# Autocorrelation decoder layer: the top-8 weights chosen by comparison with the raw correlation, with the order of the pair pipeline rewritten

## What is computed

```
qf, kf = fft(q), fft(k)                      # over the 64 positions
corr = ifft(qf * conj(kf)).real              # 64 lags for each head and channel
w, idx = top_k(corr, 8)                      # int(2 * log(64)) = 8
w = softmax(w)
out = sum_i w_i * v[min(idx_i + pos, L - 1)]
x = layernorm(x + out)
...
e = clip(floor(log2(max(|v|, 2**-10))), 0, 2); step = 2 ** (e - 1)
q = clip(round(|v| / step) * step, 0, 6) * sign(v)
```

## Time and profile before

| | |
|---|---|
| median of 3 executions | 321.19 us (321.08 to 324.42) |
| the profiled execution | 323.65 us |
| its span, first to last instruction | 321.6 us |
| TensorE busy, share | 274.6 us, 85% |
| VectorE | 269.8 us, 84% |
| ScalarE | 231.1 us, 72% |
| GpSimd | 174.7 us, 54% |
| mean granted TensorE clock | 0.978 |

### The profile page before, as it was taken

One profiled execution on the slowest core, in us unless ns is written; L12 is line 12 of the kernel. 1 busy time (PEld: TensorE's weight loads), 2 busy tenths in 40 slices (PEclk: granted clock), 3 DMA queues, 4 the chain that ended last, 5 costly groups with the idle time before them and its releaser, 6 DMA issues.

```text
span 321.6 us, 4437 instructions
## 1 busy us (share of the span) xinstructions
PE 274.6 (85%) x1060; PEld 109.8 (34%) x1060; DVE 269.8 (84%) x871; ACT 231.1 (72%) x541; POOL 174.7 (54%) x226
## 2 busy tenths in 40 slices
...
GB/s 207 396 273 354 325 160 213 128 23 65 36 33 85 78 0 17 116 1 2 2 0 16 17 14 6 50 49 18 51 34 51 51 16 51 34 50 49 51 82 99
DMA packets 22576, 26.54 MB, mean 83 GB/s; under 512 B 10771, under 2 KB 11411, under 8 KB 22550
## 3 DMA queue, kind: packets, MB, share of 16 engines
...
...
## 4 chain that ended last, share of the span: by engine, by line
DVE 30%; ACT 20%; PE 18%; issue 15%; POOL 11%; DMA 3%; SPq 1%; POOLq 0%; DVEq 0%; ACTq 0%
DVE big L1172 5%; DVE m L1153 4%; DVE X L1107 3%; DVE big L1142 3%; DMA big<-in_xT_dram 3%; PE ps L380 3%; ACT big L654 3%; DVE ps L1203 3%; ACT L752 2%; DVE ps L1081 2%; ACT X L682 2%; PE ps L562 2%; POOL big L925 2%; POOL big L931 2%; DVE big L1277 2%
## 5 line engine op out<-in xcount | busy, mean ns | idle before, releaser
L654 ACT ACTIVATE big<-X,lnv 128x512 f32<-128x512 f32 x48 | 34.2, 713 | 15.0 <-DVE X L1107 15.0
L1107 DVE SCALAR_TENSOR_TENSOR X<-ps,X 128x512 f32<-128x512 f32 x48 | 32.1, 682 | 10.7 <-PE ps L415 6.1
L391 PE MATMUL ps<-ctx_ring,consts 64*128 64x512 f32 (+1 forms) x96 | 35.8, 643 | 0.0
L441 PEld LDWEIGHTS ps<-consts,big 96*128 96x128 f32 x256 | 29.8, 191 | 13.4 <-issue 10.6
L441 PE MATMUL ps<-consts,big 96*128 96x64 f32 x256 | 32.0, 278 | 1.1 <-DVE big L1142 1.1
L1184 DVE TENSOR_TENSOR big<-ps,ctxf 128x512 f32<-128x512 f32 x48 | 30.8, 683 | 2.0 <-PE ps L475 1.3
L682 ACT ACTIVATE X<-X,lnv 128x512 f32<-128x512 f32 x32 | 25.8, 808 | 0.6
L1172 DVE MATCH_REPLACE8 big<-w,big 128x64 f32<-128x64 f32 x128 | 25.1, 210 | 0.0
L838 POOL TENSOR_TENSOR big<-big 128x512 f32<-128x512 f32 x4 | 5.8, 1444 | 35.5 <-DVE big L1250 25.5
L918 POOL TENSOR_TENSOR big<-big 128x512 f32<-128x512 f32 x15 | 19.0, 1268 | 6.2 <-DVE big L1172 6.0
L1142 DVE TENSOR_TENSOR big<-ps,ctxf 96x512 f32<-96x512 f32 x32 | 20.4, 677 | 0.8 <-PE ps L428 0.8
...
## 6 DMA issues: line engine op xcount, KB each, us to landing
...
```

The source lines that it names most:

```text
L391: mm(bank(LANE_BANK[lane]), mat((CY_0, CY_1, CY_C)[f])[half, :], ctx_ring[half, r * N:(r + 1) * N], start=True, stop=True).then_inc(s_cfor ...
L441: last = mm(ps[:, 2 * N + j * P + b * L:2 * N + j * P + (b + 1) * L], PQ[0:EVEN, b * N + j * P:b * N + (j + 1) * P], mat(IC_E)[0:EVEN, 0:L ...
L654: squared[k, n] = chain(a(JUNK[k], row(n), ACT.Square, bias=st[:, 0:1], scale=-float(V), accum_out=st[:, 2:3]))
L1107: stt(row(m), bank(b), 0.0, row(m), ALU.add, ALU.add, accum_out=st[:, 0:1]).then_inc(s_sum[k], 1)
```

## The change

The two loops in the diff are those of TensorE and GpSimd. The maxima and the mask now come from the raw correlation. match_replace reads CR and m8 instead of G and w8 and writes TAKEN (-3e38) where one of the 8 maxima stands; it can run before the exponentials. GpSimd no longer subtracts anything from G: it only negates the shift, and ScalarE takes exp(CR - shift) in eight instructions of 64 columns, one a group, with the shift as bias. VectorE forms WN as (REST == TAKEN) * G in one scalar_tensor_tensor. Of the rounding, the exponent mask stays on VectorE, now a tensor_tensor with a broadcast column `field` from SBUF to SBUF, and the maximum and product with MAGIC move to GpSimd. w8 goes. All the loops are written in a new order with other offsets, and with another list of idle products.

```diff
-DRAIN_BUSY = ((0, 4), (6, 6), (5, 3))
+DRAIN_BUSY = {LAST + 6: 10, LAST + 7: 12}
+TAKEN = -3.0e38
+EXPONENT = 0x7F800000
...
+            for t in range(1, PAIRS + 9):
+                out_rest(t - 6)
+                weights_to_time(t - 5)
+                out_even(t - 6)
+                weight_rest_forms(t - 5)
+                weight_forms(t - 5)
+                projection(t)
...
+                correlation(t - 3)
+                quantized_to_channels(t - 8)
+                feed_forward(t - 8)
+                query_forms(t - 2)
+                if t in DRAIN_BUSY:
+                    pe.wait_ge(s_sum[0], PAIRS)
+                    kept_busy(DRAIN_BUSY[t])
...
-                    a(w8[:, :], w8[:, :], ACT.Exp).then_inc(s_g, 1)
-                    a(G, G, ACT.Exp).then_inc(s_g, 1)
+                    for g in range(NG):
+                        last = a(G[:, g * L:(g + 1) * L], CR[n % 2][:, g * L:(g + 1) * L], ACT.Exp,
+                                 bias=den[:, 3 * NG + g:3 * NG + g + 1])
+                    last.then_inc(s_g, 1)
...
-                    chain(g_.tensor_tensor(groups(w8[:, :], TOP), top, sh.broadcast_to([P, NG, TOP]), ALU.subtract))
-                    g_.tensor_tensor(groups(G, L), groups(CR[n % 2], L), sh.broadcast_to([P, NG, L]),
-                                     ALU.subtract).then_inc(s_gs, 1)
+                    g_.tensor_scalar(den[:, 3 * NG:4 * NG], sh, -1.0, None, ALU.mult).then_inc(s_gs, 1)
...
-                    g_.tensor_tensor(WN, G, REST, ALU.subtract).then_inc(s_wn, 1)
...
+                    pool.wait_ge(s_expo, n + 1)
+                    chain(g_.tensor_scalar(MB, MB, 0.25, MAGIC, ALU.max, ALU.mult))
...
+            for t in range(PAIRS + 9):
+                block_scaled(t - 4)
+                finished(t - 9)
+                differences(t - 1)
+                clamped(t - 4)
+                rounded_off(t - 4)
                 top_differences(t)
...
-                        last = v_.match_replace(REST[:, g * L:(g + 1) * L], w8[:, g * TOP:(g + 1) * TOP],
-                                                G[:, g * L:(g + 1) * L], 0.0)
+                        last = v_.match_replace(REST[:, g * L:(g + 1) * L], top[:, g * TOP:(g + 1) * TOP],
+                                                CR[n % 2][:, g * L:(g + 1) * L], TAKEN)
...
-                    do(ts(bank(1).bitcast(I32), VB.bitcast(I32), 0x7F800000, None, ALU.bitwise_and))
-                    ts(MB, bank(1), 0.25, MAGIC, ALU.max, ALU.mult).then_inc(s_magic[1], 1)
+                    tt(MB.bitcast(I32), VB.bitcast(I32), field[:, 0:1].broadcast_to([P, V]), ALU.bitwise_and
+                       ).then_inc(s_expo, 1)
...
+                    stt(WN, REST, TAKEN, G, ALU.is_equal, ALU.mult).then_inc(s_wn, 1)
```

More of the change, by code:

```diff
@@ L355, in stored @@
                     sp.dma_start(pair_rows(out, n // 2, n % 2), row(n)).then_inc(s_store, 16)
-            for n in range(PAIRS + 3):
+            for n in range(PAIRS + 5):
                 quantized_to_channels(n)
-                stored(n - 3)
+                stored(n - 5)
             sp.wait_ge(s_store, 16 * PAIRS)
@@ L773, in weight_channels @@
                 a(wqT[:, :].rearrange("p (c n) -> p c n", c=VC)[:, :, bass.ts(l, P)],
-                  bank(4 if l == VC - 1 else 2).bitcast(BF16)[:, 0:V].rearrange("p (c n) -> p c n", c=VC), ACT.Copy).then_inc(s_qe[0], 1)
+                  bank(7 if l == VC - 1 else 2).bitcast(BF16)[:, 0:V].rearrange("p (c n) -> p c n", c=VC), ACT.Copy).then_inc(s_qe[0], 1)
             for m in range(SLOTS + 1):
                 slot(m)
-            for t in range(PAIRS + 10):
-                squares(0, t)
-                corr_out(t - 3)
-                if t == 3:
-                    weight_channels(VC - 1)
-                squares(2, t - 9)
-                if t == 2:
+            for t in range(PAIRS + 8):
+                if t == 1:
                     act.wait_ge(s_mlp, SLOTS)
                     a(SQ_LAST, XC[1], ACT.Square, bias=base[:, DEPTH:DEPTH + 1]).then_inc(s_sq1, 1)
-                quantized_out(t - 7)
-                factors(0, t - 1)
-                top_exponentials(t - 3)
-                weights_out(t - 4)
-                log_sum(t - 3)
-                normalise(0, t - 1)
-                last_factors(t - 9)
-                squares(1, t - 5)
-                factors(1, t - 5)
-                normalise(1, t - 5)
-                if t == 4:
+                squares(0, t)
+                probabilities(t - 3)
+                corr_out(t - 2)
+                last_factors(t - 8)
+                factors(0, t)
+                weights_out(t - 3)
+                top_exponentials(t - 2)
+                normalise(0, t)
+                if t == 1:
+                    weight_channels(VC - 1)
+                log_sum(t - 2)
+                quantized_out(t - 7)
+                squares(2, t - 7)
+                squares(1, t - 4)
+                factors(1, t - 4)
+                if t == 3:
                     act.wait_ge(s_var1, SLOTS + 2)
@@ L1286, in _ @@
             for t in range(PAIRS + 9):
-                attended(t)
-                weight_products(t - 6)
-                block_scales(t - 7)
-                without_largest(t - 5)
-                last_chosen(t - 5)
-                fed(t - 9)
-                last_quantized(t - 7)
-                largest(t - 4)
-                if t == 6:
+                top_sum(t - 4)
+                crossed(t - 6)
+                exponents(t - 7)
+                last_quantized(t - 7)
+                largest_taken(t - 4)
+                weight_products(t - 5)
+                block_scales(t - 6)
+                attended(t)
+                if t == 5:
                     last_norm(1, RS_LAST)
-                rounding(t - 7)
-                top_sum(t - 4)
-                query_products(t - 3)
-                crossed(t - 6)
+                chosen(t - 4)
+                largest(t - 3)
+                fed(t - 8)
+                query_products(t - 2)
 def kernel(**inputs):
```

97 lines of the change are left out of this document (34 added, 63 removed).

## The result

The changed kernel takes 330.97 us (median of 4 executions, 330.06 to 331.92) against 321.24 for the kernel before, measured beside it: ratio 1.0279, 95% interval [1.0204, 1.0353]. It is slower; 316.6 was forecast. The profiled execution took 330.10 with a span of 328.2, 6.6 more than before.

The account below looks back on a forecast made before the run. A loop VectorE, ScalarE, VectorE was taken to bound the step at 9.94 us. Terms of -2.3, -2.8, -3.65 and +4.2 along four landmarks sum to -4.6, hence 316.6 from 321.19; range 311 to 324.

Parts of the forecast that it names:

- GpSimd ... I count nothing in full steps.: GpSimd in full steps: at 8.8 of 9.9 us a step it was no bound, so its changed instructions cost nothing.
- 1.22 for both: VectorE's step: the new exponents and chosen cost 1.22 us together, 0.61 each to the next start.
- the 0.29 of contention: VectorE beside GpSimd: two-input instructions colliding add 0.29 us, kept for the range and not in the central forecast.
- my 9.63: VectorE's own work in a full step after the change: 9.63 us, from 9.73 - 1.32 + 1.22.
- the later rows of the table: Stretches behind crossed(1): to crossed(12) forecast -2.8 us, then to crossed(15) -3.65, then to the end +4.2.
- The new loop: Full step, VectorE to ScalarE's exponentials and back to chosen: 9.86 us, so a step of 9.85.
- the block maximum's wait gone: VectorE's full step: crossed comes some 4.6 us ahead of the block maximum, so ScalarE's 3.3 fit and the wait goes.
- 12 idle products: TensorE's drain: 12 matmuls of kept_busy before the last pair's transposes, taken as 4.0 us.
- the fill: Start to crossed(1): pair 0's work stands a step earlier, gain 2.3 us, with some 1.5 to either side.
- Half rate for two SBUF sources: Rival, chosen on VectorE: it costs 1.22 us (+0.53) in some 11 steps, +5.8, 322.4; chance 0.12.
- The slower rival: Chosen costs 1.22 us and also collides with GpSimd (+0.29): step 10.67, time 325.6; chance 0.10.
- The signs named for being wrong: L1205 over 1 us, a step above 10 or below 9.7, or the last transposes waiting for VectorE.

Follow-up runs that it names:

- m_forms: Changed kernel plus nine scratch 128x512 tensor_scalar at GpSimd's start, one per operation pair: (max, mult) took 1.94 us, three pairs 0.62, the others 1.5 to 2.2.
- m_collide: Measurement ahead of the program's own work, GpSimd and VectorE alone and together: VectorE's two-input tensor_tensor 0.69 us alone, 1.20 together; GpSimd's tensor_scalar 0.62 and 0.97.
- f_fast_order: f_fast with GpSimd's finished moved from ahead of differences to behind clamped: 328.85 us, ratio 1.0191, step 10.12.
- f_fast: Changed kernel with GpSimd's L918 (max, multiply) written as two cheap tensor_scalar, (min, max) and (mult, add): 326.67 us, ratio 1.0119, step 10.11.
- g_swap_order: f_fast_order with largest (eight MAX8) put ahead of chosen on VectorE: 337.62 us, ratio 1.0447, step 10.45.

## Why the prediction was wrong

- **The step that failed: "GpSimd ... I count nothing in full steps."** I counted busy shares (8.8 of 9.9) and priced the new tensor_scalar like its neighbour. From start to start before's step is 9.67 of GpSimd's work; without chosen (1.37), the two subtractions (1.25), with L910 (0.20) and one more tensor_scalar at 0.70 it would be 7.95. Measured are 10.43 and a wait of 0.19. The 2.48 between are L918 1.20, finished 0.47, L909 0.42, the dequantisation 0.25 and L920 0.13. The first is the pair's price (m_forms); the others run longer beside VectorE's two-input instructions (m_collide shows such an effect, and f_fast_order takes finished back to 0.76 by moving it; each single share was not tested).
- **With it failed a term of VectorE: "1.22 for both".** I kept the 0.29 of contention for the range, though GpSimd is busy 88% of the step. In the full step chosen takes 1.34 to the next start and exponents 0.94, together 1.06 more, which brings my 9.63 to 10.69 (10.61 measured). Both stretches end with a GpSimd instruction, and f_fast, an edit of GpSimd alone, takes 0.5 off chosen and off the step. So the bound is the loop over both engines, with L918 in it, and neither engine alone.
- **The same engine makes the later rows of the table.** From 270 to 302 us GpSimd runs without a wait and VectorE waits, and the chain is GpSimd's (L926 19.0%, L918 17.8% of it). The matmuls of feed_forward(14) start 13.45 behind crossed(15), not 10.1: the exponents start 2.98 behind it (1.6 forecast) and the way from there takes 10.47 (8.43 forecast), with L918 at 1.91 in it.
- **The new loop was right as a mechanism and small in size.** It closes the step while GpSimd has room: 9.86 in f_fast while chosen takes 0.69, 10.01 in after and 10.12 in f_fast_order, where chosen is held for 0.15 and 0.26. I had MAX8 wait for chosen alone; in g_swap_order it waits for the copy behind the exponentials. With a full step of 10.0 and all else as forecast the time would be some 1.7 higher (11 steps), still a gain: the loss comes with GpSimd's instructions.
- **What held:** L714 at 0.24 apart (2.01 for eight), the block maximum's wait gone, 12 idle products of 3.95, 2.15 and 5.5 from the last transposes on for 2.2 and 5.8, the fill within 1.1.
- **Rivals.** Half rate for two SBUF sources is not what happens: chosen's form takes 0.69 alone (m_collide), like a tensor_tensor and like the residuals with one input from PSUM. So here the measurement stands against the half throughput that the Vector Engine (DVE) Microarchitecture Reference, "7. Points that are easy to get wrong", of the Trainium skill states for this form. The slower rival came nearest, with 10.67 for the step and 1.51 for chosen (10.61 and 1.41 measured), but by luck in the split: half rate adds nothing, contention 0.72 instead of 0.29. It had 325.6, since it left the fill and the drain as forecast; no rival had GpSimd's own instructions in a bound, and so the range ended at 324. The signs named for being wrong, L1205 over 1 us and a step above 10, both came.
- **Where the expected gain went.** With the pair made cheap the change is at 326.7; with the exponentials merged, and the shift left out, at 323.0, which can't be told from before. The shortest step of any run, 9.76, is 0.19 under before's, 2 us in 11 steps: there was little to win in the full steps. No version that was run beat the kernel before.
